# State space layer on Trainium2: the positive part of the time step on VectorE instead of ScalarE

## What is computed

```
xc = silu(conv(x @ in_proj_x) + conv_b)            # 4 taps in time
dbc = xc @ x_proj                                   # 8 for the time step, 16 for B, 16 for C
dt = softplus(dbc[..., :8] @ dt_w + dt_b)
dA = exp(dt[..., None] * A)
dBx = (dt * xc)[..., None] * B[:, :, None, :]
h_t = dA_t * h_{t-1} + dBx_t                        # the scan, per channel and state
y = sum_s(h_t * C_t) + Dp * xc
out = (y * silu(z)) @ out_w + out_b                 # then residual, normalisation
```

## Time and profile before

| what | us |
|---|---|
| median of 3 runs | 3880.18 |
| lowest and highest | 3868.65, 3884.69 |
| profiled execution | 3872.9 |
| its span | 3871.1 |
| TensorE busy in the span | 3157.2 (82%) |
| VectorE busy | 2993.0 (77%) |
| ScalarE busy | 2599.1 (67%) |
| GpSimd busy | 2375.2 (61%) |

### The profile page before, as it was taken

How to read it: one execution, slowest core, us unless ns; L and a number is a source line. 1 busy time by engine, 2 the same in 40 slices (tenths; PEclk the granted TensorE clock), 3 DMA queues, 4 the chain that set the end, 5 groups by cost and what they waited for, 6 DMA issues and landing times. The chain is left out here.

```text
span 3871.1 us, 82456 instructions
## 1 busy us (share of the span) xinstructions
PE 3157.2 (82%) x29152; PEld 2179.9 (56%) x29152; DVE 2993.0 (77%) x5896; ACT 2599.1 (67%) x5235; POOL 2375.2 (61%) x2879
## 2 busy tenths in 40 slices
PE   7999579999999999999987777688848866578486
PEld 3776346666666666666665454366636533357355
DVE  3999569999999999999998466389958763178754
ACT  4888389999999999999995210166756463077562
POOL 2899478898998988888884000168755230044850
PEclk7999689999999999999999567777768877789698
DMA  3000100000000000000000512500000013500424
GB/s 93 24 24 26 48 7 13 24 24 23 24 22 20 19 23 24 24 23 24 23 18 21 141 46 93 201 29 23 12 6 1 1 25 122 208 5 1 117 59 125
DMA packets 271006, 172.53 MB, mean 45 GB/s; under 512 B 41648, under 2 KB 249976, under 8 KB 268536
## 3 DMA queue, kind: packets, MB, share of 16 engines
q1 hardware_dynamic: 270600, 167.25, 15.1%
HBM read 116.59 MB, written 50.60 MB: 43 GB/s over the span
## 5 line engine op out<-in xcount | busy, mean ns | idle before, releaser
L1223 DVE TENSOR_TENSOR_SCAN mam_hs<-mam_dA,mam_ps_b 128x1024 f32<-128x1024 f32 x512 | 1141.6, 2271 | 83.7 <-issue 43.8
L1143 ACT ACTIVATE mam_dA<-mam_dt,mam_A 128x496 f32<-128x496 f32 x1024 | 658.7, 710 | 0.4
L1005 PE MATMUL mam_ps_h<-mam_ident,mam_hs 128*128 128x128 f32 x4096 | 548.9, 277 | 64.0 <-ACT mam_hTb L1151 36.0
L1005 PEld LDWEIGHTS mam_ps_h<-mam_ident,mam_hs 128*128 128x128 f32 x4096 | 453.3, 142 | 229.2 <-issue 150.7
L1151 ACT COPY mam_hTb<-mam_ps_h 128x512 f32<-128x512 f32 x768 | 423.7, 588 | 95.9 <-PE mam_ps_h L1005 95.9
L991 PE MATMUL mam_ps_b<-mam_DB,mam_dtxt 32*128 32x512 f32 x2048 | 292.1, 637 | 78.1 <-DVE mam_hs L1223 74.0
L1017 PEld LDWEIGHTS mam_ps_y<-mam_hTb,mam_WC 128*32 128x32 f32 x8192 | 209.0, 110 | 133.1 <-issue 124.3
L1017 PE MATMUL mam_ps_y<-mam_hTb,mam_WC 128*32 128x128 f32 x8192 | 276.7, 276 | 0.3 <-issue 0.3
L774 POOL TENSOR_TENSOR mam_cv<-mam_cv,mam_tap 128x512 f32<-128x512 f32 x180 | 238.9, 1327 | 14.1
L810 POOL TENSOR_TENSOR mam_WC<-mam_cp,mam_m 128x128 f32<-128x128 f32 x512 | 194.3, 410 | 19.9 <-POOL mam_cv L774 14.8
L1233 DVE COPY mam_hTb<-mam_ps_h 128x512 f32<-128x512 f32 x256 | 174.3, 681 | 37.3 <-PE mam_ps_h L1005 35.4
(11 more groups left out here) (721 smaller groups left out, 8280.3 us busy)
## 6 DMA issues: line engine op xcount, KB each, us to landing
moe_wg<-in_L_ffn_weight SPq DMA_DIRECT2D x32, 1024.0 KB, 8.2
rnn_xr<-x SPq DMA_DIRECT2D x23, 512.0 KB, 6.3
l1y_wh<-mode_weights SPq DMA_DIRECT2D x16, 544.0 KB, 3.8
gat_hg<-in_x SPq DMA_DIRECT2D x16, 512.0 KB, 7.2
h<-gat_out SPq DMA_DIRECT2D x32, 256.0 KB, 2.3
mam_ht<-h SPq DMA_DIRECT2D x128, 64.0 KB, 2.0
mam_hr<-h SPq DMA_DIRECT2D x128, 64.0 KB, 2.0
mam_xt<-in_x SPq DMA_DIRECT2D x128, 64.0 KB, 2.1
```

Of the source, the lines that this page charges most:

```text
L1005: last = pe.transpose(ps_h[n][:, q * P:(q + 1) * P], hs[:, w % 3, c:c + P], ident[:, :])
L1143: act.activation(dA[:, h, :, n, 1:], dt[:, i % 2, h, :].rearrange("p (q t) -> p q t", q=Q)[:, :, 1:], ACT.Exp, scale=A[:, h, n:n + 1]).the ...
L1223: dve.tensor_tensor_scan(hs[:, w % 3, :], dA[:, h, first:first + 2, :, :].rearrange("p q s t -> p (q s t)"), ps_b[:, 2 * (w % 2):2 * (w % ...
```

## The change

The relu leaves ScalarE. A new function `positive` on VectorE computes the same value with one `tensor_scalar`: it adds the bias and takes the maximum with 0, from `ps_0` into `dt`, and gives `dt_read`. It waits for a new semaphore `abs_read`, which the absolute value on ScalarE now gives, so that the two engines read the bank one after the other. ScalarE's exponential waits for the same semaphore, where before it waited for a step of ScalarE's own chain. `positive` stands at u = 13 and u = 15 of the VectorE loop, behind the scan and the copy of the states and in front of the moments and the scale.

```
                     act.wait_ge(dt_ready, n - 1)
                 if i >= 2:
                     act.wait_ge(dx1_done if h else dx0_done, i - 1)
-                step.mark(act.activation(e[:, h, :], ps_0[:, :], ACT.Abs, bias=dtb[:, h:h + 1]))
-                act.activation(dt[:, i % 2, h, :], ps_0[:, :], ACT.Relu, bias=dtb[:, h:h + 1]).then_inc(dt_read, 1)
-                step.join()
+                act.activation(e[:, h, :], ps_0[:, :], ACT.Abs, bias=dtb[:, h:h + 1]).then_inc(abs_read, 1)
+                act.wait_ge(abs_read, n + 1)
                 act.activation(e[:, h, :], e[:, h, :], ACT.Exp, scale=-1.0).then_inc(e_ready, 1)
...
+            def positive(i, h):
+                n = 2 * i + h
+                dve.wait_ge(abs_read, n + 1)
+                if i >= 1:
+                    dve.wait_ge(dt_ready, n - 1)
+                if i >= 2:
+                    dve.wait_ge(dx1_done if h else dx0_done, i - 1)
+                TS(dt[:, i % 2, h, :], ps_0[:, :], dtb[:, h:h + 1], 0.0, ALU.add, ALU.max).then_inc(dt_read, 1)
...
+                if u in (13, 15) and turn(k + 2):
+                    positive(k + 2, (u - 13) // 2)
                 if u == 13 and turn(k - 1):
                     moments(k - 1)
                 if u == 15 and turn(k - 1):
```

More of the change, by code:

```diff
@@ L665, in mamba @@
         (loaded, made, prepared, folded, turned, hT_ready, xc_done, xc_ready, conv_first, conv_ready, cols_in, xs_ready, gate_done, sz_ready,
-         bc_done, bc_ready, dt_made, dt_read, e_ready, e1_ready, ln_ready, plus_ready, rest_ready, dt_ready, dtx_ready, cp_done,
+         bc_done, bc_ready, dt_made, dt_read, abs_read, e_ready, e1_ready, ln_ready, plus_ready, rest_ready, dt_ready, dtx_ready, cp_done,
          cp_ready, dx0_done, dx0_ready, dx1_done, dx1_ready, DB_ready, WC_ready, dA_ready, b_done, scanned, flipped,
@@ L671, in mamba @@
                 "loaded", "made", "prepared", "folded", "turned", "hT_ready", "xc_done", "xc_ready", "conv_first", "conv_ready", "cols_in",
-                "xs_ready", "gate_done", "sz_ready", "bc_done", "bc_ready", "dt_made", "dt_read", "e_ready", "e1_ready",
+                "xs_ready", "gate_done", "sz_ready", "bc_done", "bc_ready", "dt_made", "dt_read", "abs_read", "e_ready", "e1_ready",
                 "ln_ready", "plus_ready", "rest_ready", "dt_ready", "dtx_ready", "cp_done", "cp_ready", "dx0_done", "dx0_ready",
```

## The result

| kernel | median us | runs | lowest to highest |
|---|---|---|---|
| before | 3878.07 | 6 | 3868.65 to 3884.69 |
| after | 3891.97 | 6 | 3885.30 to 3896.74 |

The changed kernel is slower by a little: after over before is 1.0038, with a 95% interval of 1.0023 to 1.0053. The medians differ by 13.9 us. The forecast was 15.0 us more and 3895. The profiled execution after took 3896.74 us (span 3895.0), the one before 3872.9 (span 3871.1); the difference of these two, 23.8, is larger than that of the medians because each stands near an end of its own scatter. In the traces the stretch from the first scan's start to the last scan's end is 1604.2 us before and 1622.5 after, 18.3 more; the other 5.6 stand outside the scans, where no code changed.

What follows compares the result with a forecast made beforehand. No engine alone bounds the kernel, but a ring of handovers over TensorE, ScalarE and GpSimd, 50.39 us a turn. L903 0.51 late times 29.4 turns is 15.0 us, on a median of 3880.2 gives 3895; range 3874 to 3908.

Steps and rivals of the forecast that it cites:

- The first handover: Step 13: VectorE frees the bank after half 0's positive part, so TensorE's turning of time steps starts 0.42 us late.
- rival 2: Dear handover: positive part takes 0.74, release reaches TensorE after 0.15; 0.75 us a turn, 22 us, 3902; chance 0.22.
- The queue's share: VectorE's queue: each new instruction holds back the next by 0.61 us, 1.22 a turn.
- The second handover: Step 15: positive part ends at 1213.93, turning starts at 1214.02, where TensorE alone would be there at 1213.61.
- L903: TensorE's first projection of the turn, forecast to start 0.51 us late, lengthening each turn by 0.51.
- The relief of ScalarE: Two relus of 0.688 us leave ScalarE: first worth nothing, second at most 0.32 a turn, 9.4 us.
- The step that failed: Second half, VectorE: the scale behind the positive part takes 1.19 us, and 1.49 of idle time pays for it.
- the head: VectorE's stretch from step 13's b-matmuls through copy, positive part and scale to the first scan; before, 9.68 us.
- chain B: Not in forecast: VectorE's path from step 13's b-matmuls via first scan to the next b-matmuls; before, 9.68 + 40.71 us.
- chain A: The forecast's ring: b-matmuls, L903, copy, convolution, second silu, TensorE's turned states, b-matmuls; before, 50.39 us a turn.
- Rival 3: VectorE becomes the bound: 1.22 us more work a turn on the fullest engine, up to 36 us, 3916; chance 0.05.

Runs made afterwards that it cites:

- e9_late_signal: Kernel before, relus still on ScalarE, but half 0's bank release given by a one-column VectorE memset behind its moments; ratio to before 1.0018, turn 50.74 us.
- e4_half0_early: Kernel before with only half 0's positive part on VectorE, in front of the copy of states; ratio to before 0.9998, turn 50.38 us.
- e2_half1: Kernel before with only half 1's positive part on VectorE (step 15), half 0's relu on ScalarE; ratio to before 1.0003, turn 50.45 us.
- e1_half0: Kernel before with only half 0's positive part on VectorE (step 13), half 1's relu on ScalarE; ratio to before 1.0051, turn 50.84 us.
- e3_early: Kernel after with both positive parts in front of the copy of states instead of behind it; ratio to before 1.0044, turn 50.87 us.
- e6_sums_first: Kernel after with TensorE's sums put in front of the turning of time steps; ratio to before 1.0032, turn 50.78 us.
- e8_split_scale: e6_sums_first with two of the four scale instructions in front of step 15's copy of states; ratio to before 0.9994, turn 50.19 us.
- e11_early_split: e3_early with two of the four scale instructions ahead of the second positive part; ratio to before 0.9994, turn 50.37 us.
- e12_spread_ahead: e8_split_scale with GpSimd's spreading of C for group 2 moved in front of the first convolution; 3864.71 us, ratio to before 0.9959.
- e5_plain_scale: Kernel after with the four scale instructions replaced by one plain multiplication, normalisation left out; ratio to before 1.0075, turn 51.35 us.

## Why the prediction was right, and where it was not

The time, its sign and the mechanism, a bank handed back late in front of a full stretch of TensorE, held. One step failed without showing in the sum.

- **The first handover.** Forecast: L954 0.42 late. Measured: 1.56 - 1.07 = 0.49. Two terms were small. The new instruction takes 742 ns and not 0.68: it is as dear as the form with a scalar pointer, rival 2's value. And VectorE's release reaches TensorE 0.10 after the instruction's end (1214.63 + 0.74 = 1215.37, L954 at 1215.47), with 0.09 forecast and 0.15 in rival 2. e9_late_signal shows that this lateness is dear by itself, and e4_half0_early that the instruction without it is free.
- **The queue's share.** Forecast 0.61 for each; the next instruction starts 0.66 after (1214.63 to 1215.29, 1221.37 to 1222.03).
- **The second handover.** Forecast as part of the 0.51. In it the second added 0.09 at L903. L954 stands 1.56 behind its b-matmuls like the first, 0.36 later than before; e2_half1 gives it 0.13 at L903 and 0.06 a turn.
- **L903.** Forecast 0.51 late; measured 0.59, with 0.07 given back by the faster pair of L903. The turn is 0.55 longer and not 0.51. The steady turns give 16.2 us; the medians 13.9.
- **The relief of ScalarE.** Forecast: the first relu is worth nothing, and without the second L903 follows L954 by 2.53 and not 2.72. Measured: 2.50 (1222.21 to 1224.71), so the relief gives back 0.22 of the 0.36 of the second handover. The rest of it is only longer waits: ScalarE's in front of the copies of the states rises from 95.9 in the earlier trace rows to 136.0, GpSimd's in front of the convolution from 1.22 to 1.49.
- **The step that failed** is the last of the second half: "the scale behind it on VectorE takes 1.19 ... VectorE's 1.49 of idle time pays for it". It takes 2.40. The cover was 1.49, the positive part took 0.66 of it, and from the scale's start to the scan's it is now 2.32 where scale and wait together were 2.68 (1212.83 to 1215.51): 0.30 too much. With that, and with the copy 0.46 late (6.85 behind the b-matmuls, 6.39 before), the head is 0.76 longer, and chain B became as long as chain A. The growth of the scale (5.9 turns x 1.21 = 7.1 us in the window) also covers the difference between VectorE's busy 291.3 us and the 287 of the forecast. I had priced the scale by the row before without asking what stands beside it on GpSimd.
- **Rival 3**, VectorE as the bound, got 0.05 and came half true. In the kernel after both chains end within some 0.05 of each other. The second did not show in the time because the two are not added: e1_half0, with chain A alone, loses 0.45 and e2_half1 0.06, together 0.51 of the 0.55. Of the kernels with both halves on VectorE, e3_early and e6_sums_first free chain A and still lose 0.48 and 0.39, since each also delays VectorE's copy; those that shorten both chains, e8_split_scale and e11_early_split, are back at the time before. That chain B stopped short of lengthening the turn further was luck: the forecast had no term for it.

So the forecast's sum was near for a reason that is true but not the whole one. From it one would have advised to move the positive parts up. e3_early moves both and gains 0.07 a turn, because the second then waits for the absolute value. The first alone moved up, with the second left behind the copy, wasn't run. From the rows of e4_half0_early, where the early first half leaves the head at 9.68, and e2_half1, where the late second half gives 9.97 + 40.48, an estimate for it is a turn of 50.45, nearly the time before.

What stays open: the medians of e9_late_signal give half of what its turns say, within its interval. In the four traces compared here (before, after, e9_late_signal, e12_spread_ahead) the span without the stretch of the scans, where no code differs, goes from 2266.9 to 2274.7 us, so scatter of this size comes from outside the scans. And since chain B also starts from TensorE's b-matmuls, some 0.4 of both chains' delay in the kernel after is one and the same lateness, that of the first handover.

## What to carry to other kernels

An instruction that frees a buffer is priced by when it ends and who waits, and not by how long it takes: the same 0.74 us cost 0.45 a turn at one place and nothing 0.75 us earlier. Idle time that is to cover added work must also cover what the delayed neighbours turn into, so look at what runs beside them on the other engines at their new time. And where a fix for the cause that you can see brings nothing, look for a second chain of the same length, also one that the fix itself has lengthened, before the explanation is thrown away.

## What the runs showed of the hardware

**A short fp32 instruction of VectorE, SBUF to SBUF, is held by GpSimd's.** The scale is four instructions of 128x128. One of them in the kernel after, and GpSimd beside it:

```profile
1222.28 1.31 DVE L1281 TENSOR_SCALAR mam_out<-mam_z,mam_mv,mam_rstd 128x128 f32<-128x128 f32 x1
```

```profile
1222.19 1.32 POOL L782 TENSOR_TENSOR mam_dt<-mam_dt,mam_e 128x512 f32<-128x512 f32 x1
```

L782 ends at 1222.19 + 1.32 = 1223.51, and this instruction, of 0.34 elsewhere, ends at 1223.59, 0.08 behind it. The next one, beside GpSimd's L784, takes 0.65; why that much wasn't followed up. In e1_half0 it is the fourth that is caught, though by the rows it starts 0.02 before L782:

```profile
1213.84 1.39 DVE L1283 TENSOR_SCALAR mam_out<-mam_z,mam_mv,mam_rstd 128x128 f32<-128x128 f32 x1
```

```profile
1213.86 1.29 POOL L782 TENSOR_TENSOR mam_dt<-mam_dt,mam_e 128x512 f32<-128x512 f32 x1 [0.28 <-issue]
```

In the kernel before the fourth starts 0.19 ahead of L782 and takes 0.34:

```profile
1213.69 0.34 DVE L1273 TENSOR_SCALAR mam_out<-mam_z,mam_mv,mam_rstd 128x128 f32<-128x128 f32 x1
```

```profile
1213.88 1.29 POOL L782 TENSOR_TENSOR mam_dt<-mam_dt,mam_e 128x512 f32<-128x512 f32 x1 [0.45 <-issue]
```

A shift of 0.17 between two engines made a difference of 1.05 us to one instruction. This is no single case: 11 of the traces have such an instruction of 1.28 to 1.40 us, 29 times each, and every one ends 0.08 to 0.09 behind an L782. In the kernel before and in e9_late_signal none of the 128 takes over 0.43. The other way round, in e5_plain_scale, GpSimd's L773 starts 0.02 behind VectorE's L1239 and takes 1.58, where it takes 1.06 at other places of the turn: 0.52 more, beside 0.68 of L1239.

The Trainium skill, on its page "SBUF — State Buffer", section "SBUF: two separate sides", says that VectorE and GpSimd share one pair of ports. An instruction of VectorE takes it if it runs in a mode with two ports, or if it has two inputs in SBUF and GpSimd's reads SBUF; whichever of the two engines starts first holds the pair for the whole instruction, and the other is blocked. The traces agree for the scale, whose end follows L782's by 0.08, but for the 0.02 in e1_half0, by which the recorded starts are the other way round. No row shows in which mode the scale runs. For L773 they agree in the main: it meets an instruction with two inputs in SBUF and loses 0.52 of that one's 0.68. With that rule the longer scale could have been suspected; the forecast didn't use it.

**A tensor_scalar out of PSUM** with a pointer for its scalar takes 742 ns for 512 columns, 61 more than the plain copy, though it has one tensor in only.
